# Cross-attention and FFN kernel: the z of the second up-projection batch made in the output projection, and turned by 32x32 blocks instead of on TensorE

## The chip, the cores and the metric

The kernel runs on one core of one Trainium2 chip. The metric is the device time of one execution in microseconds (us); lower is better. The engines are named as in the profile: PE (TensorE), DVE (VectorE), ACT (ScalarE), POOL (GpSimd), SP (SyncE).

## What is computed

`x` is 4 batches of 512 rows of 1024 numbers, `ctx` 4 batches of 64 rows. All is float32. First a cross-attention over the normalized `x` and the context is added to `x`; the result, x1, goes through a feed-forward part with a shared path and a routed path, and is added again:

```python
x1 = x + attention(layernorm(x), ctx) @ Wo.T
z  = layernorm(x1)                       # what this change is about
logits = z @ gate_w;  w = sum(top_k(logits, 2))
h  = relu(z @ up_w) ** 2                 # up-projection, 1024 -> 2048
xl = z @ fc1_w                           # 1024 -> 512
y  = h @ down_w + (xl @ expert_w) * w @ fc2_w
out = x1 + layernorm(y, gamma, beta)
```

## The kernel before, in words

Each float32 product is made of three matmuls of a high and a low part (`parts3`, lines 116 to 120): the high part is a copy rounded to the matmul format, made by ACT; the low part is what is left, by POOL or DVE. The program runs in stages on all engines: projections of q, k and v (a), attention (b), output projection (c), up-projection with gate and fc1 (d), down-projection (e). Engines order themselves by semaphores that are waited for by hand; `past(s, v)` is a semaphore with the credit it was given at the start. The order on each engine is the order of the code.

**Output projection (c).** 16 tiles n = 4b + t of 128 rows, on PE 12 steps of 6 matmuls each. The attention's output of one tile comes in 4 units of 3 steps: SP loads unit u of tile n (`c_load_unit`, line 1425) as soon as PE has used unit u of tile n - 1, ACT makes the high part (`c_units_hi`, 1482), POOL the low part (`c_units_lo`, 1487). After the tile DVE adds x to the product (`c_dve`, 1587), into the one buffer `XR`; SP then stores the sum as x1 (1459), waits until it has landed, loads x for the next tile into the same buffer (1438), and only then goes on to the unit loads of the next tile. In the last batch (b = 3) SP, ACT and POOL also load and split the first weights of the up-projection ("jobs", `JOBS_C`, lines 1257, 1268 and 1273).

**Up-projection (d).** 4 batches, 7 groups (0 to 6) of 2 or 3 chunks of 128 output columns. For each chunk PE runs 8 steps k over z, turned so that its 1024 columns lie on the partitions. After group 0 come 16 gate matmuls (1685, 1686), after group 1 a transpose of the gate's result, for which DVE has to have copied that result (1784) behind the group's evacuations by ACT (1732). In batch 0 the jobs go on between the groups (`JOBS_FIRST`); five of them stand ahead of the evacuation of group 0.

**How z comes about** (`norm_z`, lines 132 to 247, bound to names `d_...` in line 1323). `d_load` reads x1 of a batch (2 MB) into `XN2`, issued on ACT's queue (157); `d_norm` and `d_sqrt` make the normalized rows in place (DVE 181 to 209, ACT 225). Then there are two ways to turn it:
- on PE, `d_pet0` (line 232): 4 transposes of 128x128 for each k, between the matmuls of group 6 of the batch before. Only batch 1 uses it, called in `mm_groups` from `body(0, False, True)`.
- by blocks: `d_z_out` stores z to memory (`z_scratch`, 2 MB, line 1337), `d_blocks_in` reads it back into the same place (`XB`) in 32 transfers of 64 KB so that 32x32 blocks lie right (1345), and `d_turn` lets DVE transpose the blocks into PSUM (1353). Batch 0 (in stage c), 2 and 3 use it.
In both ways ACT then makes the high part (`d_hi`, 241) and DVE the low part (`d_lo`, 245). For batch 0 that happens in tiles n = 13 to 15 of the output projection.

## Time and profile before

| what | us |
|---|---|
| median of 3 runs | 2104.98 |
| lowest, highest | 2104.34, 2106.26 |
| the profiled execution's own time | 2105.41 |
| its span in the trace | 2103.6 |

| engine | busy us | share |
|---|---|---|
| PE matmul | 2078.6 | 99% |
| PE weight load | 1732.7 | 82% |
| DVE | 802.3 | 38% |
| POOL | 753.6 | 36% |
| ACT | 693.2 | 33% |

The span is the trace from the first to the last instruction; the execution's own time is 1.8 us more. A timeline row has a start in us from the start of the span, a duration, the engine, the line, the operation and its tiles; in brackets stands the idle time before it and what ended it. Matmuls overlap, so the distance between starts tells their pace. "SPq" and "ACTq" are DMA issues by SP and ACT; their time is that of issuing, and the landing comes later.

### The profile page before, as it was taken

To read this page: it belongs to the slowest core of one execution; us is meant where nothing else is said; L and a number is where in the kernel's file an instruction comes from. 1 tells how busy PE (TensorE), PEld (TensorE's weight loads), DVE (VectorE), ACT (ScalarE), POOL (GpSimd) and SP (SyncE) were. 2 spreads that over 40 slices of the span, in tenths; PEclk is the share of its full clock that TensorE was granted. 3 is DMA by queue.
4 is the path that set the end of the run, shared out by engine and by line. 5 is a ranking of instruction groups with operands and counts; after the bars stand their busy time and mean duration, and the time that the engine had idled before them with its cause. 6 is when DMAs were issued, how large, how long until landed. Compare 5 with 4: busy or idle time off the path is not lost.

```text
span 2103.6 us, 30256 instructions
## 1 busy us (share of the span) xinstructions
PE 2078.6 (99%) x9564; PEld 1732.7 (82%) x9564; DVE 802.3 (38%) x1426; ACT 693.2 (33%) x1206; POOL 753.6 (36%) x616
## 2 busy tenths in 40 slices
PE   8999999999999999999999999999999999999998
PEld 7888888878888888878888878787878888888886
DVE  4231312178888888821102213213231332222223
ACT  5121111157777777741111223112123311111111
POOL 2533030147877777662112343010024322212221
PEclk9999999999999999999999999999999999999999
DMA  6743433625655655544346453353434622222222
GB/s 197 261 160 140 160 116 105 185 75 146 159 150 149 159 153 142 125 126 142 132 154 189 144 167 125 106 145 114 133 98 135 209 89 85 90 90 85 82 78 68
DMA packets 285330, 282.17 MB, mean 134 GB/s; under 512 B 129984, under 2 KB 197568, under 8 KB 284352
## 3 DMA queue, kind: packets, MB, share of 16 engines
q1 hardware_dynamic: 188128, 196.58, 30.2%
q10 hardware_dynamic: 97120, 84.56, 14.0%
q8 instruction: 44, 0.72, 0.1%
q14 instruction: 38, 0.31, 0.1%
HBM read 182.22 MB, written 98.58 MB: 133 GB/s over the span
## 4 chain that ended last, share of the span: by engine, by line
PE 96%; DVE 1%; DMA 1%; SPq 1%; ACT 0%; issue 0%; POOL 0%; ACTq 0%; DVEq 0%; POOLq 0%
PE psum L118 30%; PE psum L119 30%; PE psum L120 30%; PE psum L982 3%; PE psum L1028 1%; PE psum L1029 1%; PE psum L1009 1%; PE psum L1010 1%; PE psum L1686 0%; PE psum L232 0%; PE psum L1685 0%; DMA staging<-in_x 0%; DMA operands<-o_scratch 0%; SPq L796 0%; DVE small L181 0%
## 5 line engine op out<-in xcount | busy, mean ns | idle before, releaser
L118 PE MATMUL psum<-operands 128*128 128x512 f32 (+3 forms) x2888 | 1113.4, 386 | 10.6 <-DVE operands L353 10.3
L119 PE MATMUL psum<-operands 128*128 128x512 f32 (+3 forms) x2888 | 1110.8, 385 | 0.0
L120 PE MATMUL psum<-operands 128*128 128x512 f32 (+3 forms) x2888 | 1108.2, 384 | 0.0
L118 PEld LDWEIGHTS psum<-operands 128*128 128x128 f32 (+1 forms) x2888 | 543.3, 188 | 109.9 <-DVE operands L353 10.1
L120 PEld LDWEIGHTS psum<-operands 128*128 128x128 f32 (+1 forms) x2888 | 543.8, 188 | 106.2
L119 PEld LDWEIGHTS psum<-operands 128*128 128x128 f32 (+1 forms) x2888 | 544.3, 188 | 94.6
L1273 POOL TENSOR_TENSOR operands<-staging,operands 128x512 fp32r<-128x512 f32 x92 | 118.8, 1302 | 357.8 <-ACT operands L1268 357.5
L1154 DVE TENSOR_REDUCE small<-psum 128x1 fp32r<-128x576 f32 x256 | 192.9, 754 | 88.2 <-PE psum L982 88.1
L1925 POOL TENSOR_TENSOR operands<-operands 128x640 fp32r<-128x640 f32 x64 | 100.5, 1576 | 319.1 <-ACT operands L1920 319.1
L903 POOL TENSOR_TENSOR operands<-staging,operands 128x512 fp32r<-128x512 f32 x128 | 164.5, 1293 | 33.5 <-ACT operands L1076 24.7
L1776 DVE TENSOR_TENSOR staging<-staging 128x512 f32<-128x512 f32 x64 | 47.7, 765 | 307.3 <-ACT staging L1732 306.5
L1920 ACT ACTIVATE operands<-operands 128x640 fp32r<-128x640 f32 x64 | 47.4, 740 | 282.1 <-DMA operands<-h_scratch 282.1
L1487 POOL TENSOR_TENSOR operands<-operands 128x384 fp32r<-128x384 f32 x64 | 65.4, 1030 | 180.6 <-ACT operands L1482 180.0
L1069 ACT ACTIVATE staging<-psum 128x512 f32<-128x512 f32 (+1 forms) x192 | 109.2, 588 | 29.5 <-DVE psum L1182 23.7
L1268 ACT ACTIVATE operands<-staging 128x512 fp32r<-128x512 f32 x92 | 56.2, 630 | 185.8 <-DMA staging<-in_up_w 65.6
L982 PEld LDWEIGHTS psum<-operands 96*128 96x128 f32 x512 | 95.4, 189 | 25.8 <-DVE small L1154 4.7
L1076 ACT ACTIVATE operands<-staging 128x512 fp32r<-128x512 f32 (+1 forms) x192 | 112.9, 620 | 0.0
L982 PE MATMUL psum<-operands 96*128 96x288 f32 x512 | 110.3, 297 | 2.5 <-DVE small L1154 2.4
L905 POOL TENSOR_TENSOR operands<-staging,operands 64x512 fp32r<-64x512 f32 x64 | 82.5, 1288 | 62.1 <-ACT operands L1076 58.7
L637 DVE SCALAR_TENSOR_TENSOR staging<-psum,staging 128x512 fp32r<-128x512 f32 (+1 forms) x40 | 26.5, 662 | 189.0 <-ACT staging L632 189.0
L1065 ACT ACTIVATE psum<-psum 128x512 f32<-128x512 f32 x128 | 74.5, 582 | 65.9 <-PE psum L120 61.4
L1173 DVE CAST operands<-psum 128x512 fp32r<-128x512 f32 x128 | 87.2, 681 | 12.5 <-ACT psum L1065 8.3
(112 smaller groups left out, 1234.8 us busy)
## 6 DMA issues: line engine op xcount, KB each, us to landing
h_scratch<-staging ACTq DMA_DIRECT2D x80, 256.0 KB, 2.2
operands<-h_scratch SPq DMA_DIRECT2D x64, 320.0 KB, 3.1
operands<-recip_scratch SPq DMA_DIRECT2D x64, 192.0 KB, 4.3
o_scratch<-staging SPq DMA_DIRECT2D x64, 192.0 KB, 5.0
operands<-o_scratch SPq DMA_DIRECT2D x64, 192.0 KB, 2.7
operands<-q_hi_scratch ACTq DMA_DIRECT2D x14, 768.0 KB, 5.9
operands<-q_lo_scratch ACTq DMA_DIRECT2D x14, 768.0 KB, 6.1
staging<-in_x SPq DMA_DIRECT2D x20, 512.0 KB, 4.1
```

The lines of the kernel that those rows point to most:

```text
L118: e.matmul(o, lh, rh, start=first, stop=False)
L119: e.matmul(o, lh, rl, start=False, stop=False)
L120: return e.matmul(o, ll, rh, start=False, stop=last)
L903: e.tensor_tensor(pt[j][1], pst[j // 2], raw(pt[j][0]), ALU.subtract).then_inc(b_lop, 1)
L905: e.tensor_tensor(pt[j][0][C:P], pst[j // 2][0:C], raw(pt[j][0][0:C]), ALU.subtract).then_inc(b_lop, 1)
L982: m = e.matmul(bank[:, h * TH:(h + 1) * TH], qp[p][0][0:HD, a * S + u * P:a * S + (u + 1) * P], kp[p][0][0:HD, h * TH:(h + 1) * TH], start ...
L1069: e.activation(pst[j // 2][0:n], bank[0:n], ACT.Exp).then_inc(b_ex, 1)
L1076: e.activation(pt[j][0][0:n], pst[j // 2][0:n], ACT.Copy).then_inc(b_hia, 1)
L1154: e.tensor_reduce(nm[o % 2][:, u:u + 1], bank[:, 0:T], AX.X, ALU.max, negate=True).then_inc(b_mx, 1)
L1173: e.tensor_copy(pt[j][0], s_bank[(o * NT + j) % 4]).then_inc(b_hid, 1)
L1273: e.tensor_tensor(job_part(j, h, slot_lo), halves[h], raw(job_part(j, h, slot_hi)), ALU.subtract).then_inc(j_lo, 1)
L1925: e.tensor_tensor(eu[u][1], raw(eu[u][1]), raw(eu[u][0]), ALU.subtract).then_inc(e_lo, 1)
```

## The change

The z of batch 1 now goes by blocks too, and most of it in stage c. For this all of batch 0's steps stand one tile earlier there: the load of x1 between the units of n = 9, the root ahead of n = 10, the norm behind the add of n = 8, the store behind n = 10, the block reads in n = 11 and 12, the high parts in n = 14, and DVE's adds of n = 13 and n = 14 in the places that n = 14 and n = 15 had. Behind the last high part of z 0, ahead of the units of n = 15, ACT issues the load of batch 1's x1; root, norm and store of batch 1 stand in n = 15. The block reads of batch 1 go between the first eight jobs of the up-projection, four transfers behind each. In group 6 of batch 0 the transposes on PE go away, and DVE turns blocks there as in the later batches. The load, root and norm that stood in batch 0's groups are gone from there.

```diff
--- before.py
+++ after.py
@@ -1325,9 +1325,6 @@
             "d", XN2, lambda e, b: e.wait_ge(*past(d_acc, b * ND)))
 
 
-        def nth_z(b):
-            return 1 if isinstance(b, int) and b == 0 else b
-
         XB = SF[:, D:D + ST * D].rearrange("p (k s) -> p k s", k=DK)
         d_zs, d_bl = sem("d_z_stored"), [sem(f"d_blocks_loaded{h}") for h in range(2)]
 
@@ -1339,7 +1336,7 @@
         def d_blocks_in(e, b, h, ks=range(4)):
 
             if h == 0 and ks[0] == 0:
-                e.wait_ge(*past(d_zs, nth_z(b) * 16))
+                e.wait_ge(*past(d_zs, b * 16 + 16))
             for k in [4 * h + k for k in ks]:
                 for g in range(P // 32):
                     e.dma_start(XB[32 * g:32 * g + 32, k, :].rearrange("p (u j) -> p u j", j=32),
@@ -1348,7 +1345,7 @@
         def d_turn(e, b, k):
 
             if k % 4 == 0:
-                e.wait_ge(*past(d_bl[k // 4], nth_z(b) * (4 * 64)))
+                e.wait_ge(*past(d_bl[k // 4], b * (4 * 64) + 4 * 64))
             e.wait_ge(*past(d_zl, b * DK + k - 1))
             e.transpose(PS[:, 6 + k % 2, :], XB[:, k, :]).then_inc(d_zt, 1)
 
@@ -1487,20 +1484,28 @@
                 e.tensor_tensor(cu[u][1], raw(cu[u][1]), raw(cu[u][0]), ALU.subtract).then_inc(cc_lo, 1)
 
         def c_act(e):
+            FROM = (FB + 1) * ST + 3
+
             def tiles(b, jobs=None):
                 m = 0
                 for t in range(ST):
                     n = b * ST + t
                     if b == FB and t == 0:
                         f_expert_hi(e)
-                    if jobs and t == 3:
+                    if b == FB + 1 and t == 2:
+                        d_sqrt(e, 0)
+                    if jobs and t == 2:
                         d_hi(e, 0, 0)
                         d_hi(e, 0, 1)
                     if n:
                         c_units_hi(e, n, (0, 1))
-                    if jobs and t < 2:
-                        d_blocks_in(e, 0, t, (0, 1))
-                    if jobs and t == 3:
+                    if b == FB + 1 and t == 1:
+                        e.wait_ge(*past(cc_st, ST * 16))
+                        e.wait_ge(*past(f_st, NQ * 16))
+                        d_load(e, x1_d, 0)
+                    if n in (FROM, FROM + 1):
+                        d_blocks_in(e, 0, n - FROM, (0, 1))
+                    if jobs and t == 2:
                         d_hi(e, 0, 2)
                         d_hi(e, 0, 3)
                     for j in (jobs or {}).get(t - 1, []):
@@ -1508,28 +1513,28 @@
                         m += 1
                     if n:
                         c_units_hi(e, n, (2, 3))
-                    if jobs and t < 2:
-                        d_blocks_in(e, 0, t, (2, 3))
+                    if n in (FROM, FROM + 1):
+                        d_blocks_in(e, 0, n - FROM, (2, 3))
                     if b == FB:
                         f_fc2_hi(e, t)
                         if t:
                             f_evac(e, t - 1)
                     if b == FB + 1 and t == 0:
                         f_evac(e, NQ - 1)
-                    if b == FB + 1 and t == 1:
-                        e.wait_ge(*past(cc_st, ST * 16))
-                        e.wait_ge(*past(f_st, NQ * 16))
-                        d_load(e, x1_d, 0)
                     if b == FB + 1 and t == 2:
-                        d_sqrt(e, 0)
-                    if b == FB + 1 and t == 3:
                         d_z_out(e, 0)
+                    if jobs and t == 2:
+                        for k in range(4, DK):
+                            d_hi(e, 0, k)
+                        e.wait_ge(*past(cc_st, 2 * ST * 16))
+                        d_load(e, x1_d, 1)
+                    if jobs and t == 3:
+                        d_sqrt(e, 1)
+                        d_z_out(e, 1)
 
             for b in range(B - 1):
                 tiles(b)
             tiles(B - 1, JOBS_C)
-            for k in range(4, DK):
-                d_hi(e, 0, k)
 
         def c_pool(e):
             def tiles(b, jobs=None):
@@ -1593,18 +1598,19 @@
                             f_expert_lo(e)
                         f_fc2_lo(e, t)
                     tile(b, t)
-                    if b == FB + 1 and t == 1:
+                    if b == FB + 1 and t == 0:
                         d_norm(e, 0)
             tile(B - 1, 0)
-            tile(B - 1, 1)
             d_turn(e, 0, 0)
             d_turn(e, 0, 1)
             for k in range(DK):
                 if k == DK - 2:
-                    tile(B - 1, 2)
+                    tile(B - 1, 1)
                 d_lo(e, 0, k)
                 if k + 2 < DK:
                     d_turn(e, 0, k + 2)
+            tile(B - 1, 2)
+            d_norm(e, 1)
             tile(B - 1, 3)
 
 
@@ -1658,12 +1664,7 @@
                         run(r, jobs_of(r)[1])
 
         def d_pe(e):
-            def pet(e, b, k):
-                if k == 0:
-                    e.wait_ge(*past(d_gc, b * GC))
-                d_pet0(e, b, k)
-
-            def body(b, last, first=False):
+            def body(b, last):
                 def wait_bank(g, c):
                     if g == 0:
                         e.wait_ge(*past(d_ev, b * ND - 2 + c))
@@ -1690,11 +1691,10 @@
                         e.sem_inc(idle, 1)
                         e.transpose(PS[:, 6, 0:P], gTs, ident[:]).then_inc(d_gt, 1)
 
-                mm_groups(e, b, D_GROUPS, d_zl, wait_bank, job_slot, d_acc, slot_ready, gate, d_fr, pet if first else None)
+                mm_groups(e, b, D_GROUPS, d_zl, wait_bank, job_slot, d_acc, slot_ready, gate, d_fr)
 
             e.wait_ge(*past(cc_x1, B * ST - 1))
-            body(0, False, True)
-            with e.Fori(1, B - 1) as b:
+            with e.Fori(0, B - 1) as b:
                 body(b, False)
             body(B - 1, True)
 
@@ -1715,6 +1715,8 @@
                         elif at == -1:
                             free = lambda: e.wait_ge(*past(cc_use, B * ST * 4))
                         job_hi(e, j, m0 + m[0], free)
+                        if isinstance(b, int) and b == 0 and m[0] < DK:
+                            d_blocks_in(e, 1, m[0] // 4, (m[0] % 4,))
                         m[0] += 1
 
                 run(-1, b)
@@ -1749,9 +1751,7 @@
                     if g in (3, 4) and not last and not first:
                         d_blocks_in(e, b + 1, g - 3)
                     run(g, b)
-                    if g == 0 and first:
-                        d_load(e, x1_d, b + 1)
-                    if g == (2 if first else 1) and not last:
+                    if g == 1 and not last and not first:
                         d_sqrt(e, b + 1)
 
             body(0, False, True)
@@ -1764,11 +1764,11 @@
                 n = 0
                 for g, chunks in enumerate(D_GROUPS):
                     final = g == len(D_GROUPS) - 1 and not last
-                    for k in range(2 if final and not first else 0):
+                    for k in range(2 if final else 0):
                         d_turn(e, b + 1, k)
                     for k in range(DK - 1 if final else 0):
                         d_lo(e, b + 1, k)
-                        if k + 2 < DK and not first:
+                        if k + 2 < DK:
                             d_turn(e, b + 1, k + 2)
                     for c, ch in enumerate(chunks):
                         if ch[0] == "u":
@@ -1800,7 +1800,7 @@
                             link(e.max(gtop[:, t, :], g8[:, t, :]))
                         link(e.tensor_tensor(rw[:, bass.ds(b * ST, ST)], gtop[:, :, 0], gtop[:, :, 1], ALU.add))
                         assert q[0] == GC
-                    if g == (2 if first else 1) and not last:
+                    if g == 1 and not last and not first:
                         d_norm(e, b + 1)
 
             e.wait_ge(*past(d_gw, 16))
```

How this moves instructions. **ACT in tiles n = 14 and 15** (line 1482, in the change 1479, is a unit's high part, 241 a high part of z, 1268 a weight's, 157 the 2 MB load). Before, from the units of n = 14 on:

```order
L1482 ACTIVATE operands<-operands 128x384 [waits c_o_loaded2]
L1482 ACTIVATE operands<-operands 128x384 [waits c_o_loaded3]
L241 ACTIVATE operands<-psum 128x512 [waits d_zfree,d_zt] x2
L1482 ACTIVATE operands<-operands 128x384 [waits c_o_loaded0]
L1482 ACTIVATE operands<-operands 128x384 [waits c_o_loaded1]
L241 ACTIVATE operands<-psum 128x512 [waits d_zfree,d_zt] x2
L1268 ACTIVATE operands<-staging 128x512 [waits job_raw0]
L1268 ACTIVATE operands<-staging 128x512 [waits job_raw1]
L1482 ACTIVATE operands<-operands 128x384 [waits c_o_loaded2]
L1482 ACTIVATE operands<-operands 128x384 [waits c_o_loaded3]
L241 ACTIVATE operands<-psum 128x512 [waits d_zfree,d_zt] x3
L241 ACTIVATE operands<-psum 128x512 [waits d_product,d_zt]
```

Now, from k = 2 of z on, the first unit row again being of n = 14:

```order
L241 ACTIVATE operands<-psum 128x512 [waits d_zfree,d_zt] x2
L1268 ACTIVATE operands<-staging 128x512 [waits job_raw0]
L1268 ACTIVATE operands<-staging 128x512 [waits job_raw1]
L1268 ACTIVATE operands<-staging 128x512 [waits job_raw0]
L1268 ACTIVATE operands<-staging 128x512 [waits job_raw1]
L1479 ACTIVATE operands<-operands 128x384 [waits c_o_loaded2]
L1479 ACTIVATE operands<-operands 128x384 [waits c_o_loaded3]
L241 ACTIVATE operands<-psum 128x512 [waits d_zfree,d_zt] x3
L241 ACTIVATE operands<-psum 128x512 [waits d_product,d_zt]
L157 DMA staging<-x1_scratch 128x4x1024 [waits c_stored,d_zt]
L1479 ACTIVATE operands<-operands 128x384 [waits c_o_loaded0]
L1479 ACTIVATE operands<-operands 128x384 [waits c_o_loaded1]
```

The high parts k = 4 to 7 now stand right behind the units of n = 14, and the 2 MB load between them and the first unit of n = 15.

**DVE at the end of the turns of z 0** (line 1353, now 1350, turns; 245 is a low part; 1587, now 1592, the add of a tile). Before:

```order
L245 TENSOR_TENSOR operands<-psum,operands 128x512 [waits d_zhi]
L1353 STREAM_TRANSPOSE psum<-staging 128x512 [waits d_zlo]
L245 TENSOR_TENSOR operands<-psum,operands 128x512 [waits d_zhi]
L1353 STREAM_TRANSPOSE psum<-staging 128x512 [waits d_zlo]
L1587 TENSOR_TENSOR staging<-psum,staging 128x1024 [waits c_x_loaded,c_unit_used]
L245 TENSOR_TENSOR operands<-psum,operands 128x512 [waits d_zhi] x2
L1587 TENSOR_TENSOR staging<-psum,staging 128x1024 [waits c_x_loaded,c_unit_used]
L1807 CAST operands<-small 128x8x8 [waits d_gate_weights]
```

Now:

```order
L245 TENSOR_TENSOR operands<-psum,operands 128x512 [waits d_zhi]
L1350 STREAM_TRANSPOSE psum<-staging 128x512 [waits d_zlo]
L245 TENSOR_TENSOR operands<-psum,operands 128x512 [waits d_zhi]
L1350 STREAM_TRANSPOSE psum<-staging 128x512 [waits d_zlo]
L1592 TENSOR_TENSOR staging<-psum,staging 128x1024 [waits c_x_loaded,c_unit_used]
L245 TENSOR_TENSOR operands<-psum,operands 128x512 [waits d_zhi] x2
L1592 TENSOR_TENSOR staging<-psum,staging 128x1024 [waits c_x_loaded,c_unit_used]
L181 BN_STATS small<-staging 128x6 [waits d_x]
L181 BN_STATS small<-staging 128x6 x7
```

The rows of the turns are alike, but the add between them and the last two low parts was that of n = 14 and is now that of n = 13; the add behind it is that of n = 14, and then comes the norm of batch 1 and the add of n = 15. Four adds stand ahead of the first turn in both, those of n = 10 to 13 before, of n = 9 to 12 now.

**ACT at the start of the up-projection** (1268 is a weight's high part, 1732, now 1734, evacuates group 0). Before, the last two of the five pairs ahead of the evacuation:

```order
L1268 ACTIVATE operands<-staging 128x512 [waits job_raw0,c_unit_used]
L1268 ACTIVATE operands<-staging 128x512 [waits job_raw1]
L1268 ACTIVATE operands<-staging 128x512 [waits job_raw0,c_unit_used]
L1268 ACTIVATE operands<-staging 128x512 [waits job_raw1]
L1732 ACTIVATE staging<-psum 128x512 [waits d_stored0,d_product]
L1732 ACTIVATE staging<-psum 128x512 [waits d_stored1,d_product]
L1732 ACTIVATE staging<-psum 128x512 [waits d_stored2,d_product]
```

Now, the first two of the same five pairs, with the root and the store of batch 1's z ahead of them:

```order
L225 ACTIVATE small<-small 128x4 [waits d_chain]
L1334 DMA z_scratch<-staging 128x4x1024 [waits d_z]
L1268 ACTIVATE operands<-staging 128x512 [waits job_raw0,c_unit_used]
L1268 ACTIVATE operands<-staging 128x512 [waits job_raw1]
L1342 DMA staging<-z_scratch 32x16x32 [waits d_z_stored]
L1342 DMA staging<-z_scratch 32x16x32 x3
L1268 ACTIVATE operands<-staging 128x512 [waits job_raw0,c_unit_used]
L1268 ACTIVATE operands<-staging 128x512 [waits job_raw1]
L1342 DMA staging<-z_scratch 32x16x32 x4
```

Behind each pair of a weight's high parts stand four block reads, up to the eighth pair; the evacuation of group 0 still stands behind the fifth.

## Rows read from the trace of the kernel before

**Rows 1.** The page: busy time by engine, and the granted clock by slices

```profile
PE 2078.6 (99%) x9564; PEld 1732.7 (82%) x9564; DVE 802.3 (38%) x1426; ACT 693.2 (33%) x1206; POOL 753.6 (36%) x616
...
PEclk9999999999999999999999999999999999999999
```

**Rows 2.** The gate's matmuls (line 1685), PE, windows of batch 0, 1 and 2

```profile
L1685 PE MATMUL psum<-operands x8: 390/392/398, 1219.9 to 1223.2; 128*16 128x512 f32 x8
...
L1685 PE MATMUL psum<-operands x8: 390/392/398, 1336.4 to 1339.6; 128*16 128x512 f32 x8
...
L1685 PE MATMUL psum<-operands x8: 390/392/398, 1449.1 to 1452.3; 128*16 128x512 f32 x8
```

**Rows 3.** Timeline of PE in group 6 of batch 0 (start, duration, instruction)

```profile
1307.02 0.60 PE L232 MATMUL psum<-ident,staging 128*128 128x128 f32 x4
1307.38 0.48 PE L118 MATMUL psum<-operands 128*128 128x512 f32 x1
...
1309.55 0.60 PE L232 MATMUL psum<-ident,staging 128*128 128x128 f32 x4
```

**Rows 4.** Timeline of DVE, end of the output projection

```profile
1171.16 1.23 DVE L1587 TENSOR_TENSOR staging<-psum,staging 128x1024 f32<-128x1024 f32 x1 [15.09 <-PE psum L120]
...
1176.94 0.69 DVE L245 TENSOR_TENSOR operands<-psum,operands 128x512 fp32r<-128x512 f32 x1 [3.33 <-ACT operands L241]
...
1179.00 0.73 DVE L1353 STREAM_TRANSPOSE psum<-staging 128x512 f32<-128x512 f32 x1
...
1203.80 1.23 DVE L1587 TENSOR_TENSOR staging<-psum,staging 128x1024 f32<-128x1024 f32 x1 [7.59 <-PE psum L120]
```

**Rows 5.** Timeline of ACT, the same stretch

```profile
1175.89 0.53 ACT L1482 ACTIVATE operands<-operands 128x384 fp32r<-128x384 f32 x1 [0.51 <-DMA operands<-o_scratch]
1176.32 1.07 ACT L241 ACTIVATE operands<-psum 128x512 fp32r<-128x512 f32 x2
1181.38 1.19 ACT L1482 ACTIVATE operands<-operands 128x384 fp32r<-128x384 f32 x2 [3.99 <-DMA operands<-o_scratch]
```

**Rows 6.** Timeline of SP's DMA queue, the same stretch

```profile
1177.17 0.34 SPq L1438 DMA_DIRECT2D staging<-in_x  x1
1177.61 2.14 SPq L1425 DMA_DIRECT2D operands<-o_scratch  x2
```

**Rows 7.** DMA issues, KB, us to landing, 1086 to 1104

```profile
staging<-x_scratch ACTq DMA_DIRECT2D x1, 2048.0 KB, 9.6
...
x_scratch<-staging SPq DMA_DIRECT2D x1, 512.0 KB, 2.7
staging<-in_x SPq DMA_DIRECT2D x1, 512.0 KB, 7.5
```

**Rows 8.** Timeline of POOL, two splits of n = 15

```profile
1181.98 2.00 POOL L1487 TENSOR_TENSOR operands<-operands 128x384 fp32r<-128x384 f32 x2 [3.51 <-ACT operands L1482]
```

**Rows 9.** PE timeline at the start; PE waits from 30 us on

```profile
6.55 0.58 PE L118 MATMUL psum<-operands 128*128 128x256 f32 x1 [6.55 <-DVE operands L353]
...
10.13 0.41 PE L119 MATMUL psum<-operands 128*128 128x256 f32 x1
10.34 0.41 PE L120 MATMUL psum<-operands 128*128 128x256 f32 x1
...
11.30 0.28 PE L119 MATMUL psum<-operands 128*128 128x256 f32 x1
11.42 0.28 PE L120 MATMUL psum<-operands 128*128 128x256 f32 x1
...
PE psum L982 <- DVE small L1154: 2.4, 2, 2.2
```

**Rows 10.** ACT and DVE timelines in batch 0; landings of unit loads (line 1425)

```profile
1231.88 1.55 ACT L1732 ACTIVATE staging<-psum 128x512 f32<-128x512 f32 x3
...
1235.01 1.16 DVE L1784 COPY small<-psum 16x128 f32<-16x128 f32 x4
...
DMA to landing us min/median/max: 2.4/2.9/6.4
```

## Prediction

> **What bounds the kernel now.** I first read the page: PE is busy for 2078.6 of 2103.6 us, at a granted clock of nine tenths or more in every slice [rows 1]. So only PE work that vanishes, or a stall of PE that appears or goes, changes the time. The list of PE's waits from 30 us on has nothing longer than 2.2 us [rows 9]: there is hardly a stall to win, and the slack of the others is what can be lost. For the price of the transposes I then read the starts of the gate matmuls batch by batch, and PE's timeline in group 6 of batch 0; for the new order, the timelines of DVE, ACT and SP around tiles 13 to 15, where the reader is to see what each instruction waited for and how early it was.
>
> **Removed: 32 transposes on PE.** From the gate of batch 0 to that of batch 1 it takes 116.5 us (1219.9 to 1336.4), to that of batch 2 112.7 us [rows 2]. The same matmuls run in both; only the first stretch has the transposes: 3.8 us. The timeline agrees: four transposes and nine matmuls take 1309.55 - 1307.02 = 2.53 us [rows 3], nine matmuls alone 9 x 0.227 = 2.04 (72 matmuls of a group last 16.32), so 0.49 for each of 8 k. All of it is on PE's path: **-3.8 us**. Batch 1 to 2 already turns by blocks without a wait in that second stretch, so DVE and ACT in group 6 cost nothing; they have the same work there.
>
> **Moved: z 0 one tile earlier.** Load, norm, store and block reads delay unit loads as they did, one tile earlier, and a unit load is hidden as long as it comes before PE has used the tile before. I take 0, with up to 1 us if the store of z and x's load meet worse than before. The load, root and norm taken out of batch 0's groups free DVE and ACT, on which PE did not wait: 0.
>
> **Moved: the add of n = 13 behind the turns.** This is the term that decides. Before, that add started at 1171.16, as soon as PE was through [rows 4]. Now it stands behind the low parts k = 4 and 5 of z, which wait for ACT's high parts, and these stand behind the last unit of n = 14, whose high part ran from 1175.89 to 1176.42 [rows 5]. At this very place ACT had k = 0 and 1 before (1176.32), and DVE answered with a low part at 1176.94 and the second turn ending at 1179.73 [rows 4, 5]. The same two low parts and two turns now end about 1179.8; the add takes 1.23 us, to 1181.0, ten us later than 1171.16. PE doesn't wait for it, but SP does: it stores x1 of n = 13, waits for the landing, loads x, and only then issues the first unit of n = 15, which went out at 1177.61 [rows 6].
>
> The store now leaves at 1181.1. The 2 MB load of batch 1's x1 left ACT's queue at 1179.8, as soon as the last turn was done. For a 512 KB transfer behind such a load the trace has 7.5 us (x's load; the 2 MB took 9.6), for a store without it 2.7 [rows 7]. I take 7.5, since the distance (1.3 us there) and size are the same: landed at 1188.6. Then 0.6 for x's load and the unit's issue: 1189.2. The unit's high part started 1181.38 - 1177.61 = 3.8 us after its issue, POOL 0.6 later, 1.0 for the split [rows 5, 6, 8]: ready at 1194.6. PE wants it when tile 14 ends: the adds of n = 13 and n = 15 start 32.64 us apart, so tile 14 ends at about 1187.2, a quarter us before its add could start [rows 4]. **Stall: +7.4 us.** Bounds: with 2.7 for the store it is 2.6; if the unit's own load also falls behind the rest of the bulk, 9. Queued behind that wait on SP are the unit loads 1 to 3 and the job u3; they then go out together, and PE uses a unit in 4.1 us, so they add nothing.
>
> **PE's clock behind the stall.** At the kernel's start PE has been idle for 6.55 us; its matmuls of 256 columns then start 0.21 us apart (10.13, 10.34) and from about 10.8 on 0.12 apart (11.30, 11.42) [rows 9]. That is the lower of the two levels (1.2 GHz) for 4.3 us, then 2.4. After the longest later idle time, 2.2 us, the page's slices show no fall. A stall of 7.4 is nearer to the first case: 4.3 us at half speed, **+2.1 us**; bounds 0 and 4. The Trainium skill ("TensorE: Matmul & The Clock Gate", Part 1) says that an idle array falls to 1.2 GHz and regains 2.4 only after sustained work. By that rule the 2.1 stand; by the 2.2 us row alone they would be 0. The start agrees with the rule, and no run here yet shows a fall in mid-kernel.
>
> **Added: 32 block reads between the jobs.** Before, the evacuation of group 0 started at 1231.88 behind five jobs, and the copies of the gate's result ended at 1236.17 [rows 10]. PE wanted them after group 1, at 1219.9 + 3.6 (16 gate matmuls) + 16.3 = 1239.8: slack 3.7 us. The four issues fit ACT's idle time behind each pair. But a weight's load now meets 256 KB of 128-byte pieces. Unit loads landed in 2.4 us at best and 6.4 at worst while such reads ran [rows 10]; I take 1 us for each of the four loads that follow a block read ahead of the evacuation: 4.0 against 3.7, **+0.3 us**; bounds 0 and 3. Later groups have more slack, since batch 1's 2 MB load no longer runs there.
>
> **Sum:** -3.8 + 7.4 + 2.1 + 0.3 = +6.0 us on the profiled execution's own 2105.41: 2111.4. That execution is 0.4 above the median of 2104.98, so as a median **2111.0 us**, 0.29% slower. About 0.2% (4.2 us) is what a measurement of this kernel can tell from no change.
>
> **Rivals.**
> - *The stall comes, the clock stays.* +3.9 us, 2108.9. For it: no fall is seen after 2.2 us; against: the start. On the border of "same": 0.15, half to each side.
> - *The two queues share evenly.* The store then needs its own 512 KB and as much of the other queue; instead of 7.5 about 4 us, so the stall is about 4 and the sum near 0 to +2: 2105 to 2107. The Trainium skill ("DMA: Bandwidth & Descriptors", "Queues, rings and completion order") has each DMA engine take turns between its queues packet by packet, which speaks for this. The row of 7.5 speaks against it: x's load landed with the bulk, not ahead. 0.13.
> - *The other side: SP isn't late for PE.* From its issue the store takes at least 2.7 + 0.6 + 3.8 + 1.6 = 8.7 us to a ready unit, so it decides where the store leaves by 1178.5 and lands undisturbed. This needs ACT to reach z's high parts k = 4 and 5 some 3 us earlier, that is units 2 and 3 of n = 14 to arrive ahead of the weight loads before them. SP's order speaks against it, but the block reads that slowed these loads are gone from tile 13. Then only -3.8 remains: 2101.2. 0.07.
> - *The splits fall behind.* If a job's cycle grows by 2 us instead of 1, the gate's result is 8.0 - 3.7 = 4.3 us late, 4 more than in the forecast: up to 2115. 0.13.
> - The forecast itself: 0.52.
>
> **How the numbers follow.** Slower by over 0.2%: the forecast, the late splits and about a third of the first rival, 0.70. Faster by over 0.2% means more than -4.2 us, which even the third rival reaches only with scatter: 0.04. The rest, 0.26, is within 0.2%. For the range I leave out the third rival and the end of the late splits: from 2104.5 (even sharing with a short stall) to 2115.0 (stall 9, clock 3, splits 1.5 us).
>
> **What would show it.** In the changed kernel's trace: gates of batch 0 and 1 112.7 us apart; DVE's add of n = 13 near 1180; SP's store of x1 landing in about 7.5 us, the first unit of n = 15 issued near 1189; one idle time of PE near 1187 of about 7 us, ended by POOL's split; then matmuls of 512 columns 0.43 us apart for some us; PE idle for less than 1 us before the transpose behind group 1. I am wrong if the unit is issued by 1182, if the store lands in 3 us beside the 2 MB load, or if the matmuls after the stall start 0.227 apart at once.

## The result, and the profile after

| | median us | lowest to highest, 9 runs |
|---|---|---|
| before | 2105.40 | 2104.34 to 2110.72 |
| the change | 2111.55 | 2109.71 to 2115.21 |

The ratio is 1.0024, with a 95% interval of 1.0014 to 1.0033: 5.0 us slower (3 to 7 by the interval); the two medians alone are 6.15 us apart. The forecast was 2111.0 us and slower by 6. The profiled execution of the change took 2111.0 us, with this span and busy time on its page:

```profile
span 2109.2 us, 30252 instructions
...
PE 2078.8 (99%) x9532; PEld 1733.4 (82%) x9532; DVE 806.9 (38%) x1434; ACT 693.1 (33%) x1206; POOL 753.5 (36%) x616
```

PE has the same work less 32 transposes (9532 instructions against 9564) in a span that is 5.6 us longer. Its waits (us in total, times, the longest) show where:

```profile
PE psum L118 <- DVE operands L353: 9.4, 4, 6.1
PE psum L118 <- POOL operands L1484: 6.2, 1, 6.2
PE psum L982 <- DVE small L1154: 2.8, 1, 2.8
```

The first belongs to the start, and the last is that of [rows 9], 0.6 us longer. The middle one is new: one idle time of 6.2 us, ended by POOL's split of a unit (now line 1484). DVE's timeline, where 1592 is the add of a tile, shows how it came:

```profile
1156.35 1.22 DVE L1592 TENSOR_TENSOR staging<-psum,staging 128x1024 f32<-128x1024 f32 x1 [15.10 <-PE psum L120]
...
1177.06 0.69 DVE L245 TENSOR_TENSOR operands<-psum,operands 128x512 fp32r<-128x512 f32 x1 [6.20 <-ACT operands L241]
...
1179.76 1.20 DVE L1592 TENSOR_TENSOR staging<-psum,staging 128x1024 f32<-128x1024 f32 x1
...
1192.89 1.23 DVE L1592 TENSOR_TENSOR staging<-psum,staging 128x1024 f32<-128x1024 f32 x1 [10.74 <-DMA staging<-in_x]
```

These are the add of n = 12, the low part k = 4 of z, the add of n = 13, and that of n = 14, which waited 10.74 us for x. Against [rows 4], where the add of n = 13 followed that of n = 12 by 16.3 us, it is now 23.4 us behind. ACT's timeline has the last unit of n = 14, behind it (not shown) the high parts k = 4 to 7 from 1176.44 on, the 2 MB load leaving its queue (157), and then nothing until the first unit of n = 15:

```profile
1176.01 0.53 ACT L1479 ACTIVATE operands<-operands 128x384 fp32r<-128x384 f32 x1 [0.28 <-DMA operands<-o_scratch]
...
1179.98 0.40 ACTq L157 DMA_DIRECT2D staging<-x_scratch  x1
1193.44 1.07 ACT L1479 ACTIVATE operands<-operands 128x384 fp32r<-128x384 f32 x2 [12.96 <-DMA operands<-o_scratch]
```

SP's queue has the store of x1 (1456), the load of x (1435) and the first two units of n = 15 (1422), which in [rows 6] went out at 1177.61:

```profile
1181.05 0.36 SPq L1456 DMA_DIRECT2D x_scratch<-staging  x1
1189.35 0.34 SPq L1435 DMA_DIRECT2D staging<-in_x  x1
1189.80 0.91 SPq L1422 DMA_DIRECT2D operands<-o_scratch  x2
```

The landings of the store and, below it, of the 2 MB load:

```profile
L1456 SPq DMA_DIRECT2D x_scratch<-staging x1: 356/356/356, 1181.0 to 1181.0; - x1
...
DMA to landing us min/median/max: 8.2/8.2/8.2
...
L157 ACTq DMA_DIRECT2D staging<-x_scratch x1: 396/396/396, 1180.0 to 1180.0; - x1
...
DMA to landing us min/median/max: 9.9/9.9/9.9
```

The store took 8.2 us (a quiet one 2.7 [rows 7]), and SP stood still for it from 1181.05 to 1189.35. How it took them is seen in the packets that each queue moved (number, MB, share of the 16 DMA engines). SP's queue is q1, ACT's is q10; the first line is of 1181 to 1185, the other two of 1186 to 1187.5:

```profile
q10 hardware_dynamic: 269, 1.10, 94.8%
...
q1 hardware_dynamic: 77, 0.32, 51.0%
q10 hardware_dynamic: 76, 0.31, 50.3%
```

Up to 1185 SP's queue has no line at all: in windows of 0.1 us, the store's first packets stand in that of 1185.4, 4.4 us behind its issue. From then on the two queues move packet for packet. So of the 8.2 us the first 4.4 are a late start (0.8 us for the undisturbed store of e10_add_before_5) and the rest is sharing. PE around the stall, each row one matmul of 512 columns:

```profile
1188.57 0.39 PE L120 MATMUL psum<-operands 128*128 128x512 f32 x1
1195.18 0.76 PE L118 MATMUL psum<-operands 128*128 128x512 f32 x1 [6.23 <-POOL operands L1484]
1195.75 0.63 PE L119 MATMUL psum<-operands 128*128 128x512 f32 x1
...
1197.88 0.47 PE L118 MATMUL psum<-operands 128*128 128x512 f32 x1
1198.19 0.40 PE L119 MATMUL psum<-operands 128*128 128x512 f32 x1
1198.43 0.40 PE L120 MATMUL psum<-operands 128*128 128x512 f32 x1
```

The next matmul was due 0.23 us behind 1188.57, at 1188.80, and came at 1195.18: 6.4 us. Then the starts are 0.42 to 0.57 us apart six times, and from 1198.19 on, as the last two rows show, again 0.23 to 0.24: the six took 2.7 us instead of 1.36, with the seventh 1.4 us lost to the lower of the two clock levels. The granted clock (here 0.50, the third number from the end) says the same:

```profile
1196.00:1198.00 2.00, 2.00 (x6) 1.52 (x6) 2.00 (x4) 1.66 (x4) 1.91 (x2) 0.50 0.77 293
```

In 1199 to 1200 it is 1.00. The gates of batch 0 and batch 1, to be held against [rows 2]:

```profile
L1686 PE MATMUL psum<-operands x8: 390/392/397, 1229.3 to 1232.5; 128*16 128x512 f32 x8
...
L1686 PE MATMUL psum<-operands x8: 390/392/397, 1342.0 to 1345.2; 128*16 128x512 f32 x8
```

They are 112.7 us apart, not 116.5: the 3.8 us of the transposes are really gained. Last, the jobs of the up-projection's start, with the first and the fifth pair of high parts on ACT:

```profile
1220.05 1.24 ACT L1268 ACTIVATE operands<-staging 128x512 fp32r<-128x512 f32 x2 [19.64 <-DMA staging<-in_up_w]
...
1242.01 0.63 ACT L1268 ACTIVATE operands<-staging 128x512 fp32r<-128x512 f32 x1 [3.95 <-DMA staging<-in_up_w]
```

the copies of the gate's result on DVE:

```profile
1247.65 1.16 DVE L1784 COPY small<-psum 16x128 f32<-16x128 f32 x4
```

and the transpose behind group 1 that needs them, on PE:

```profile
L1692 PE MATMUL psum<-ident,small x1: 270/270/270, 1249.4 to 1249.4; 128*128 128x128 f32 x1
```

A job's cycle is (1242.01 - 1220.05) / 4 = 5.5 us, where it was (1229.84 - 1210.78) / 4 = 4.8. And behind the fifth pair ACT first issues four more block reads: it starts the evacuation of group 0 (line 1734) 1.4 us later for it, an idle time that the profile puts down to "issue". The copies end at 1248.8 and PE's transpose starts at 1249.4: the slack went from 3.8 us [rows 10] to 0.6, and PE did not wait.

**Summing up.** I measure from the start of the add of n = 12 to the first gate matmul of batch 1, which holds all that the change touches but the first steps of z 0. That is 181.6 us before and 1342.0 - 1156.35 = 185.6 in the change: +4.0 = -3.8 + 6.4 + 1.4. Of the 5.6 us between the spans, 1.5 lie ahead of it: the add of tile n = 1 starts at 937.4 us in the change and started at 935.9 before, so they come from the attention ahead of it, which is the same code. Most of them arise at one place, the wait of 2.8 us above; the second line is the granted clock a little behind it:

```profile
445.67 0.52 PE L982 MATMUL psum<-operands 96*128 96x288 f32 x2 [2.76 <-DVE small L1154]
...
447.10:450.00 2.90, 2.90 (x10) 2.35 (x9) 1.91 (x4) 2.14 (x4) 1.68 (x2) 0.50 0.00 0
```

In the kernel before PE waited 2.16 us there, and the granted clock of 445 to 450 is 1.00.

### The profile page after: what moved, and what is told of

Its sections match the earlier page's. It is cut to its first block, busy times and chain, and to the rows that moved or that the text cites. A ratio compares the mean times of both kernels' runs of the same rounds, so it can differ in the third digit from the quotient of the medians.

```text
span 2109.2 us, 30252 instructions
## 1 busy us (share of the span) xinstructions
PE 2078.8 (99%) x9532; PEld 1733.4 (82%) x9532; DVE 806.9 (38%) x1434; ACT 693.1 (33%) x1206; POOL 753.5 (36%) x616
## 4 chain that ended last, share of the span: by engine, by line
PE 96%; DMA 1%; DVE 1%; ACT 1%; issue 0%; SPq 0%; POOL 0%; DVEq 0%; ACTq 0%; POOLq 0%
PE psum L118 30%; PE psum L119 30%; PE psum L120 30%; PE psum L982 3%; PE psum L1028 1%; PE psum L1029 1%; PE psum L1009 1%; PE psum L1010 1%; DMA x_scratch<-staging 0%; PE psum L1687 0%; PE psum L1686 0%; DMA operands<-o_scratch 0%; DMA staging<-in_wqkv 0%; PE psum L232 0%; DMA v_lo_scratch<-staging 0%
## 5 line engine op out<-in xcount | busy, mean ns | idle before, releaser
L1069 ACT ACTIVATE staging<-psum 128x512 f32<-128x512 f32 (+1 forms) x192 | 109.2, 587 | 29.9 <-DVE psum L1182 23.4
L1076 ACT ACTIVATE operands<-staging 128x512 fp32r<-128x512 f32 (+1 forms) x192 | 112.9, 621 | 0.0
```

Source lines behind the costliest of these rows:

```text
L1069: e.activation(pst[j // 2][0:n], bank[0:n], ACT.Exp).then_inc(b_ex, 1)
L1076: e.activation(pt[j][0][0:n], pst[j // 2][0:n], ACT.Copy).then_inc(b_hia, 1)
```

## The experiments

Each ratio is taken against runs of the kernel before on the same chip in the same session. Single executions scatter by several us, nearly all of it in the attention: the add of n = 1 started between 935.0 and 944.8 us in the twelve profiles of this case (before, the change, ten experiments), with the change itself at both 937.4 and 935.0. So beside the ratio the table gives the stretch from the add of n = 12 to the gate of batch 0, on to that of batch 1, and PE's idle time at tile 15, all in us. These come from one trace of each kernel, and the sum stands against the one trace of before.

| run | PE idle at tile 15 | n = 12 to gate 0 | gate 0 to gate 1 | sum against before | ratio, 95% interval |
|---|---|---|---|---|---|
| before | 0 | 65.1 | 116.5 | 0 | |
| the change | 6.2 | 72.9 | 112.7 | +4.0 | 1.0024 (1.0014 to 1.0033) |
| e0_change | 6.6 | 74.0 | 112.7 | +5.1 | 1.0028 (1.0018 to 1.0038) |
| e1_add_early | 0 | 65.0 | 112.7 | -3.9 | 0.9982 (0.9969 to 0.9995) |
| e9_add_early_again | 0 | 65.1 | 112.9 | -3.6 | 0.9982 (0.9972 to 0.9991) |
| e2_small_load | 0.8 | 66.1 | 112.7 | -2.8 | 0.9992 (0.9979 to 1.0005) |
| e7_half_load | 4.2 | 71.1 | 113.0 | +2.5 | 1.0015 (0.9998 to 1.0032) |
| e10_add_before_5 | 4.8 | 72.9 | 113.0 | +4.3 | 1.0010 (0.9999 to 1.0020) |
| e4_reorder_only | 0.8 | 66.2 | 116.4 | +1.0 | 0.9995 (0.9984 to 1.0006) |
| e8_load_after_units | 1.2 | 66.5 | 122.8 | +7.7 | 1.0045 (1.0027 to 1.0063) |
| e5_double_reads | 0 | 65.0 | 114.3 | -2.3 | 0.9993 (0.9979 to 1.0008) |
| e6_reads_late | 0 | 65.1 | 124.1 | +7.6 | 1.0036 (1.0022 to 1.0051) |

My theory was the forecast's: the add of n = 13 behind the turns holds SP back, and the 2 MB load in front of its store makes that long. The rivals were that the load alone, the lateness alone, or the block reads do it.

**The change again (e0_change).** No edit.

> The change again, for the scatter and for its parts beside the others on one chip. Theory: an idle time of PE of 6 to 7 us at tile 15, some matmuls behind it at 0.43 us, gates of batch 0 and 1 112.7 us apart, 4 to 6 us above the kernel before. Of the 5.6 us between the two traces 1.5 lay in the attention already, which the change does not touch: if that is scatter, other runs show it with either sign; if it belongs to the change, this run shows it again.

It is as expected: 6.6 us idle, eleven matmul starts at the lower level, 5.1 us in the stretch. The store again took 8.2 us, its first packets 4.4 us behind the issue. The attention this time was 0.9 us shorter than before, so the 1.5 us above are scatter of that part.

**The add ahead of k = 4 (e1_add_early).**

```diff
-                if k == DK - 2:
+                if k == DK - 4:
                     tile(B - 1, 1)
```

> The change with DVE's add of n = 13 moved ahead of the low part k = 4 of z 0, two turns and two low parts earlier in the order; everything else as in the change. Theory (the late add holds SP back, and the unit loads of n = 15 with it): the add starts near 1171 again, its store lands before the 2 MB load leaves, PE has no idle time at tile 15 and its clock doesn't fall; what stays is the 3.8 us of the transposes, so 3.8 us less than the kernel before (ratio 0.998). Rival (the 2 MB load beside the unit loads of n = 15 is enough by itself to stall PE): an idle time of over 3 us near 1187 stays and the time is that of the kernel before or more. Rival (the extra 6 us come from the block reads between the jobs): the time stays 5 to 6 us above the kernel before.

SP's queue in this run, the store and the first two units of n = 15 (between them, at 1176.58, the load of x):

```profile
1172.59 0.36 SPq L1456 DMA_DIRECT2D x_scratch<-staging  x1
...
1177.03 2.83 SPq L1422 DMA_DIRECT2D operands<-o_scratch  x2
```

and of PE's waits from 400 us on the one that is longest in total:

```profile
PE psum L982 <- DVE small L1154: 2.5, 2, 2.0
```

The store leaves at 1172.6, before the 2 MB load (1179.2), and the first unit at 1177.0. The second unit left at 1179.5, behind the load, and took 8.8 us; PE had no need of it yet. No wait at tile 15 is left, the clock stays, and the ratio is 0.9982: the 3.8 us of the transposes and nothing else. The other two rivals fall: the 2 MB load is still there beside the later units of n = 15, and the block reads still stand between the jobs.

**The same again (e9_add_early_again).**

> The kernel of the first experiment again (the add of n = 13 ahead of the low part k = 4), on this chip: 3.8 us below the kernel before if the first comparison (ratio 0.9982) was not scatter, no idle time of PE at tile 15, gates of batch 0 and 1 112.7 us apart. If the attention's scatter of several us from execution to execution made that ratio, it comes out near 1.

0.9982 again, on another chip. This is a version that beats both kernels: 3.8 us below the one before, and about 9 below the change (9.0 by the sums of the table, 9.7 by the ratios of the first session).

**The load cut to 128 KB (e2_small_load).** Leaves out 15 of 16 columns of batch 1's x1 before its norm.

```diff
-                        d_load(e, x1_d, 1)
+                        e.wait_ge(*past(d_zt, DK))
+                        e.dma_start(XN2[:, :, 0:64], x1_d[S:2 * S, 0:64]...)
```

> The change with batch 1's 2 MB load cut to 64 of 1024 columns (128 KB), at the same place; so the output of batch 1 is computed from rows that are mostly left over from batch 0. Theory (lateness of the add costs 2.6 us, the 2 MB load in front of the store the rest): the add is as late as in the change (about 1180), the store lands in about 2.7 us instead of 8.2, the idle time of PE at tile 15 is 1.5 to 3 us instead of 6.2 and the clock stays, so the time is 1 to 2 us below the kernel before. Rival (lateness of the add is all): the idle time stays at 6 us. Rival (the load is all): no idle time at all and 3.8 us less than before.

PE's wait in this stretch:

```profile
PE psum L118 <- POOL operands L1485: 0.8, 1, 0.8
```

Idle 0.8 us, less than the 1.5 to 3 expected. The lateness of the add costs a microsecond, the 2 MB load in front of the store the other five and the clock's fall. The ratio's interval (0.9979 to 1.0005) holds both -2.8 us and nothing.

**The load cut to 1 MB (e7_half_load).** Leaves out half of batch 1's rows of x1.

```diff
-                        d_load(e, x1_d, 1)
+                        e.wait_ge(*past(d_zt, DK))
+                        e.dma_start(XN2[:, 0:2, :], x1_d[S:S + 2 * P, :]...)
```

> The change (late add) with batch 1's load cut to half of its rows, 1 MB, at the same place; so half of batch 1's rows are normalized from what batch 0 left. Theory (the store lands behind whatever bulk stands in front of it): the store lands in 5 to 6 us (2.7 with 128 KB, 8.2 with 2 MB), PE idles 3 to 4.5 us at tile 15. For the clock: nothing fell at 0.8 us of idle time and all fell at 6.2; if it falls here too, 5 to 10 matmuls behind the stall are 0.43 us apart. Rival (the size doesn't matter, two transfers always share): the store lands in 8 us as with 2 MB.

The store's landing:

```profile
L1457 SPq DMA_DIRECT2D x_scratch<-staging x1: 356/356/356, 1181.1 to 1181.1; - x1
...
DMA to landing us min/median/max: 5.8/5.8/5.8
```

and PE behind the stall:

```profile
1193.07 0.53 PE L118 MATMUL psum<-operands 128*128 128x512 f32 x1 [4.20 <-POOL operands L1485]
...
1196.79 0.39 PE L118 MATMUL psum<-operands 128*128 128x512 f32 x1
```

2.6 us with 128 KB in front, 5.8 with 1 MB, 8.2 with 2 MB: the landing grows with what stands in front. The late start does not grow in the same way: the store's first packets come 0.8 us behind its issue with 128 KB, 3.7 us with 1 MB and 4.4 us with 2 MB. With 1 MB the load is nearly through by then, and the store has the DMA engines nearly to itself. The nine starts from 1193.07 on take 3.72 us instead of 2.04, most of them 0.43 us apart, so the clock fell behind 4.2 us of idle time too.

**The add between k = 4 and 5 (e10_add_before_5).**

```diff
-                if k == DK - 2:
+                if k == DK - 3:
                     tile(B - 1, 1)
```

> The change with the add of n = 13 moved only one turn and one low part earlier, between the low parts k = 4 and 5. Theory (what counts is when the first unit of n = 15 is ready, and anything behind the 2 MB load is slow): the add starts about 1.3 us earlier than in the change (some 23.5 us behind the start of the add of n = 12... 22.1 instead of 23.4), so the store leaves ahead of the 2 MB load and lands in 3 to 5 us; but x's load and the first unit's load are then behind it and take 7 to 8 us, so PE still idles 3 to 6 us at tile 15, and the time is between that of the kernel before and 4 us above. Rival (only the store's place against the load counts): no idle time over 1 us, as with the add ahead of k = 4, and 3.8 us less than the kernel before.

This one turns the order of the store and the 2 MB load around and leaves the unit behind. On SP's queue:

```profile
1180.97 0.36 SPq L1456 DMA_DIRECT2D x_scratch<-staging  x1
1183.72 0.34 SPq L1435 DMA_DIRECT2D staging<-in_x  x1
1184.17 1.18 SPq L1422 DMA_DIRECT2D operands<-o_scratch  x2
```

the landings of x and of the four units of n = 15 (min, median, max):

```profile
L1435 SPq DMA_DIRECT2D staging<-in_x x1: 341/341/341, 1183.7 to 1183.7; - x1
...
DMA to landing us min/median/max: 8.0/8.0/8.0
...
L1422 SPq DMA_DIRECT2D operands<-o_scratch x4: 378/538/953, 1184.2 to 1190.0; - x4
...
DMA to landing us min/median/max: 6.2/8.8/8.9
```

and on ACT the 2 MB load leaving:

```profile
1182.37 0.40 ACTq L157 DMA_DIRECT2D staging<-x_scratch  x1
```

The store left at 1180.97, ahead of the load at 1182.37, and landed in 2.7 us. But x then took 8.0 us and the units 6.2 to 8.9, ACT made the first high part at 1193.00, and PE idled for 4.8 us. The lower clock level behind it lasted longer than in the change: of the 7.8 us more up to the gate, 2.8 are its share. (The ratio allows only 0 to 4.2 us in all; the one trace, +4.3, lies just above its upper end.) The load of x shows the two halves of the delay again: it was issued at 1183.72, its first packets stand at 1187.5, and in 1188 to 1190 SP's queue moved 0.37 MB beside 0.45 MB of ACT's. So it is not the store's place alone that counts: what SP issues just behind the 2 MB load, on the other queue, starts late, then shares, and lands about when that load is through. This bears out the theory and excludes the rival of this run.

**Only the move of z 0 (e4_reorder_only).** Stage c as in the change without batch 1's steps; stage d as before.

```diff
-                        e.wait_ge(*past(cc_st, 2 * ST * 16))
-                        d_load(e, x1_d, 1)
-                    if jobs and t == 3:
-                        d_sqrt(e, 1)
-                        d_z_out(e, 1)
...
-            d_norm(e, 1)
```

> Only the first half of the change: z of batch 0 one tile earlier in the output projection, with the late add of n = 13; batch 1 is turned on PE as before, with its load in batch 0's groups. Theory: no 2 MB load stands in front of the store, so it lands in about 2.7 us, PE idles 1.5 to 3 us at tile 15 with its clock unchanged, the transposes stay: 1.5 to 3 us above the kernel before. Rival (moving z 0 costs nothing by itself): the same as before within 0.5 us.

0.8 us idle and +1.0 in the stretch, with the transposes back (116.4): again less than the 1.5 to 3 expected, and by the ratio not to be told from nothing.

**The load behind the first units of n = 15 (e8_load_after_units).**

```diff
+                    if jobs and t == 3:
+                        e.wait_ge(*past(cc_st, 2 * ST * 16))
+                        d_load(e, x1_d, 1)
                     if jobs and t == 2:
                         d_hi(e, 0, 2)
```

> The change (late add) with batch 1's 2 MB load moved behind the first two units of n = 15 on ACT, so that it no longer stands in front of the store. Theory: PE idles only about 1 us at tile 15 and its clock stays; but the load lands 10 us later, the norm of batch 1 with it, and DVE's add of n = 15 stands behind that norm: SP's last store and the first jobs of the up-projection come 8 to 12 us late, and PE waits 6 to 12 us for weights and at the transpose behind group 1. So 3 to 9 us above the kernel before. Rival (moving the load is enough): 2.8 us below the kernel before, like the run with the small load.

The idle time at tile 15 is down to 1.2 us, but DVE starts the norm of batch 1 late and the add of n = 15 behind it:

```profile
1208.03 4.85 DVE L181 BATCH_NORM_STATS2 small<-staging 128x6 f32<-128x512 f32 x8 [10.40 <-DMA staging<-x_scratch]
...
1218.64 1.22 DVE L1593 TENSOR_TENSOR staging<-psum,staging 128x1024 f32<-128x1024 f32 x1
```

That add, of n = 15, is 1218.64 - 1163.77 = 54.9 us behind the one of n = 12, where it was 49.0 before, and not for PE's sake: DVE came from the norm without an idle time. PE waits later for the gate's copies and for weights:

```profile
PE psum L1693 <- DVE small L1785: 3.7, 1, 3.7
PE psum L118 <- POOLq L1275: 3.1, 1, 3.1
```

Behind both waits the starts are 0.42 to 0.43 us apart for some six matmuls, which adds about 3 us to the 6.8 of waiting. The gates are 10.1 us further apart than in the change, the sum is 7.7 above before, within the 3 to 9 expected, and all runs say 1.0045. The wait had only moved.

**Block reads twice as dense (e5_double_reads),** on the kernel with the early add.

```diff
-                        if ... and m[0] < DK:
-                            d_blocks_in(e, 1, m[0] // 4, (m[0] % 4,))
+                        if ... and m[0] < DK // 2:
+                            d_blocks_in(e, 1, m[0] // 2, (2 * m[0] % 4, 2 * m[0] % 4 + 1))
```

> The change with the early add (as in the first experiment), and batch 1's block reads packed twice as dense: eight transfers behind each of the first four jobs instead of four behind each of eight. Theory (each job's cycle grows with the reads behind it; with four it went from 4.75 to about 5.5 us and left 0.5 us of PE's slack at the transpose behind group 1): the cycles grow to about 7 us, the gate's result comes some 5 us too late, and PE idles about 5 us before that transpose: 1 to 2 us above the kernel before, 5 above the first experiment. Rival (the reads hide beside the splits): the time of the first experiment, 3.8 us below the kernel before.

PE waited 1.2 us for the gate's copies, and the stretch is 1.6 us longer than in e1_add_early. The mechanism is there, its size was overstated: cycles of 6.1 us instead of 5.4, not 7, and a stretch 2.3 us below the kernel before, not 1 to 2 above.

**Block reads in groups 3 and 4 (e6_reads_late),** on the kernel with the early add.

```diff
-                        if isinstance(b, int) and b == 0 and m[0] < DK:
-                            d_blocks_in(e, 1, m[0] // 4, (m[0] % 4,))
...
-                    if g in (3, 4) and not last and not first:
+                    if g in (3, 4) and not last:
```

> The change with the early add, and batch 1's block reads taken out from between the jobs and put behind groups 3 and 4, where the later batches have theirs. Theory: the jobs' cycle is 4.75 us again and the gate's result is 3 to 4 us early instead of 0.5, but PE did not wait there, so the time is that of the first experiment within 0.5 us (gates of batch 0 and 1 112.7 us apart). Rival (the dense reads slow PE or its feeding): 1 us or more below the first experiment. Rival (the reads behind groups 3 and 4 delay the jobs of the last groups in batch 0): PE waits in group 6, some us above.

The third reading was the right one, though the longer wait comes one step later than it had it. ACT issues 16 reads in a row twice: for 8.9 us behind group 3, and for 11.4 behind group 4. The jobs and then the evacuation of group 4 (1301.11) stand behind the first sixteen, and PE, which needs those banks in group 6, waits 1.9 us at 1302.79. Behind the second sixteen come the turns and high parts of batch 1's z, and behind these the evacuation of group 6:

```profile
1304.10 11.44 ACTq L1342 DMA_DIRECT2D staging<-z_scratch  x16
...
1326.27 1.08 ACT L1732 ACTIVATE staging<-psum 128x512 f32<-128x512 f32 x2
```

PE needs that bank for group 0 of batch 1, and waits 7.5 us:

```profile
1326.91 0.80 PE L118 MATMUL psum<-operands 128*128 128x512 f32 x1 [7.50 <-ACT staging L1732]
```

Together with a clock that falls behind the second wait (granted 0.50 in 1326.9 to 1329.6) this is nearly all of the 11.4 us that the gates are further apart than in e1_add_early. The later batches have one job behind a group instead of two or three and bear it; batch 0 does not. Where the change put the reads, one k behind each job, PE did not wait for them.

## Why the prediction was right, and where its terms were off

**The transposes, -3.8.** Exact: 112.7 us between the gates.

**z 0 one tile earlier, 0.** Right in that no unit before n = 15 came late. But it had an effect that I had named only under the third rival: with no block reads in tile 13, the units of n = 14 came sooner. The last one's high part started 1175.89 - 1154.8 = 21.1 us behind the add of n = 12 before, 1176.01 - 1156.35 = 19.7 in the change. So the add of n = 13 was 1.6 us earlier than I had it (23.4 behind that of n = 12, not 25.0).

**The stall, +7.4.** The mechanism was right step by step: low part, turn, add, store behind the 2 MB load, x, unit, split. Its size was 6.4. The 1.6 us came off, and the store took 8.2 us instead of the 7.5 read from x's load: 7.4 - 1.6 + 0.7 = 6.5. That row was a good guide because the same happens there: x's load was issued at 1093.68 and its first packets stand at 1097.4, 3.7 us later. The lower bound, 2.6 without the bulk in front, was 1.6 too high for the same reason; e2_small_load and e4_reorder_only measured 1.0.

**The clock, +2.1.** 1.4 in the change's profile, 2.2 in its repetition (1193.37 to 1198.06, eleven starts at 4.7 us instead of 2.5). The row at the start of the kernel was a fair guide, though only the pace shows the level there: the profile's granted clock is 1.00. The first rival (the clock stays) is out. What was weak is the reading against it. Forty slices of 53 us cannot show a fall of three: those of the change are all nines too. The trace can: behind the 2.2 us of the kernel before (at 445.03) the starts are 0.23 to 0.24 us apart from 445.40 on, so the clock did stay. But the length of one idle time does not decide. All of 4.2 us and more were followed by a fall, and so was one of 2.0 us in e8_load_after_units (at 749.91, granted 0.52 in the 3 us behind it), while one of 3.0 us in e5_double_reads (at 503.49) left it at 1.00. Nor does it give the price: 4.2, 4.8, 6.2 and 6.6 us cost 1.7, 2.8, 1.4 and 2.2. The Trainium skill ("TensorE: Matmul & The Clock Gate", Part 1) says that an idle array falls back to half the clock; these runs agree, with 0.43 against 0.23 us between starts.

**The block reads, +0.3.** The cycle grew by 0.7 us, not 1, and PE did not wait: 0. It was closer than the sum says, for the four issues did not all fit ACT's idle time: those behind the fifth pair held the evacuation back by 1.4 us. The rival of the late splits is out for the change; e5_double_reads shows what it would have taken.

**Even sharing of the queues.** Its price is out, its rule is not. The Trainium skill ("DMA: Bandwidth & Descriptors", "Queues, rings and completion order") has an engine take turns between its queues. The trace agrees for the time in which both queues move: 77 and 76 packets in 1186 to 1187.5. What I had worked out from that, about 4 us for the store, left out the start: a transfer on SP's queue that left ahead of the 2 MB load had its first packets 0.8 us behind the issue and landed in 2.7 us; one that left just behind it had them 3.7 to 4.4 us behind and landed in 7.5 to 8.2. What holds the start back stays open, as no run here was made for it.

**SP isn't late for PE.** It did not happen in the change, but e1_add_early made it happen, with the price that I had given it, -3.8.

**The sum.** +6.0 was forecast; the stretch that the change touches shows +4.0 in one profile and +5.1 in the other, all runs +5.0. The term that was sized too large is the stall (by 1.0), then the clock (by 0.7 in that profile) and the reads (0.3). That the median came within 0.6 us of 2111.0 is partly luck: the medians differ by 6.15 us, the ratio stands for 5.0, and the attention's scatter lies between.

## What to carry to other kernels

When an instruction is moved back in an engine's order, follow who waits for it until PE is reached: PE did not wait for this add, but SP did, which feeds PE two tiles later. When a bulk transfer is added, list what leaves behind it on every queue before it has landed, and who waits for that (a second queue did not help here: the small transfer started late all the same); here moving one add by two steps in DVE's order, past the place where a wait stood, was worth 9 us. And a stall of a few us has a second price, the matmuls at half clock behind it.

## What was not expected of the hardware

- A transfer on one queue starts late when a bulk load has just been issued on the other. A 512 KB store on SP's queue landed in 2.6, 5.8 and 8.2 us with 128 KB, 1 MB and 2 MB issued 1.1 us ahead of it on ACT's queue; its first packets came 0.8, 3.7 and 4.4 us behind its issue. Only from there on did the two queues share evenly. Four unit loads of 192 KB behind 2 MB had a median of 8.8 us, against 2.9 in [rows 10].
- The same store issued 1.4 us ahead of the bulk took 2.7 us, and issued 1.1 us behind it 8.2: which of two issues on different queues came first decided over 5.5 us of landing.
- The clock can fall behind an idle time as short as 2.0 us, and stay up behind one of 3.0.
- The attention differs by up to 10 us between executions of the same code (935.0 to 944.8 at the add of n = 1). In the four profiles that were latest there (941.0 to 944.8) it comes in one or two steps of about 3 to 5 us. Each has an idle time of PE of 2.0 to 3.5 us, ended by DVE's line 1154 or by a DMA from `small`, and all but one have matmuls at the lower clock behind them. What makes these waits longer in one execution than in another stays open, as no run here was made for it.
